# Scores ahead of the values product in each attention step of the first layer

## Chip, cores and metric

The kernel runs on one core of one Trainium2 chip. The metric is the device time of one execution in microseconds (us), lower is better. TensorE does the matrix products, ScalarE (ACT), VectorE (DVE) and GpSimd (POOL) the elementwise work, and each engine works through its own queue in program order, with semaphores between the queues.

## The reference, cut to what matters

Two layers run one after the other on x of shape (8, 32, 32, 512) in float32. The change touches only the first, a group norm, an attention with 8 heads of 64 channels over the 1024 positions of each of the 8 images, and an output projection with a residual:

```
qkv = group_norm(x) @ w_qkv + b_qkv            # (8, 1024, 1536)
weight = softmax(einsum('bhld,bhsd->bhls', q * scale, k * scale))
out = einsum('bhls,bhsd->bhld', weight, v)
x = x + out @ w_out + b_out
```

## The kernel before

`layer0` prepares weights and then runs the same block, `image`, for each of the 8 images. All products are made of pairs of a high and a low part of the float32 operands. TensorE first does the projections, then the attention, then the output projection of the image.

The attention of an image is a loop over steps `i_`. A **unit** u is 128 query rows of one head: 8 heads of 8 units, U = 64 units. Four functions issue TensorE's work:

- `scores(i_)` (L428, L429; called S here): 4 products of 512 columns into PSUM banks 2*(i_%2) and the next one. It waits for the exponentials of unit i_-2, which free these banks. At the first unit of a head it also waits for `staged`: POOL must have made the high and low parts of this head's keys and queries.
- `transposes(u)` with u = i_-2 (L443; T): 8 transposes of 128 columns, in two groups of four, into banks 4 and 5. Each group waits for `pl_ok`, which is DVE's subtraction of the group before it in the same bank.
- `output(b, part)` (L464; O): half of the values product of a pair b of units, 8 products of 256 columns. Part 0 runs in odd steps and begins with two more transposes, of the reciprocals of the row sums (L459; R). Part 1 runs in even steps and ends the pair's product (`av_ps`).

The other engines, in the order of their queues within step i_:

- ACT: in even steps two copies of the finished product of pair b = (i_-6)/2, `fold_t` (L544) and `fold_r` (L548), which wait for `av_ps`; then the high parts of the transposed probabilities of unit i_-2, `ph` (L558, two groups); then the exponentials of unit i_, `prob` (L565). In some steps a copy `ah` (L573).
- DVE: the row maximum of unit i_ (L599), which waits for its scores; in even steps the sum `fold_s` (L607), which waits for `fold_r`; the low parts `pl` of unit i_-2 (L616, two groups, each behind its `ph`); in odd steps the reciprocals (L620); in steps 23, 25, 39, 41, 55, 57 and four behind the last scores (`SPLIT_AT`) the low part `al` (L624), behind `ah`.
- POOL: for each pair the product `a_qk` (L696), behind `fold_s`. Behind this product of pairs 4k-2, 4k-1 and 4k, for k = 1 to 6, one of three parts of `stage(k + 1, ...)`. The last part, the low half of the keys `kl` (L687), follows pair 4k, so it lies in step 8k+6, and `scores(8k+8)`, the first of head k+1, waits for it:

```
for b in range(U // 2):
    pool.wait_ge(fold_add, b + 1)
    pool.tensor_tensor(qk[...], fold_s[...], fold_r[...], ALU.mult).then_inc(att_ok, 1)
    k, part = (b + 2) // NB, (b + 2) % NB
    if 1 <= k <= NH - 2 and part < 3:
        stage(k + 1, (part,))
```

(shortened; NB is 4.) SP's queue loads keys and queries of head h once the scores of head h-2 are done.

Of the kernel before, what the change touches and what calls it, by code (L numbers as in the profile page):

```python
# [80 lines left out]
def layer0(nc, x, gn_scale, gn_bias, w_qkv, b_qkv, w_out, b_out, x2, n_images=B):  # L81
    NB = TOK // 256
    U = NH * TT
    QSCALE = 1.0 / HD

    with ExitStack() as ctx:
# [275 lines left out]
        def image(i, after=None):  # L362

            with nc.Block() as block:
# [29 lines left out]
                def _(pe):  # L394

                    def projections(numbers):

                        for g in numbers:
                            if g >= 8:
                                pe.wait_ge(qk_sb, qk_upto[g - 7])  # L400
                                if v_upto[g - 7]:
                                    pe.wait_ge(vl_ok, v_upto[g - 7])
                            project(pe, g).then_inc(pr_ps, 1)

                    def turn(tiles):

                        if after is not None:
                            for t in tiles:
                                pe.wait_ge(x_ld[t], 16)
                                if t >= 4:  # L410
                                    pe.wait_ge(xt_sb, t - 3)
                                turn_tile(pe, t).then_inc(xt_ps, 1)

                    def scores(i_):

                        h, t = i_ // TT, i_ % TT
                        j = h % 2
                        if t == 0:
                            pe.wait_ge(staged, STAGE * (h + 1))
                        if i_ < 2:  # L420
                            pe.wait_ge(qk_sb, qk_upto[len(groups) - 8 + 2 * i_ + 2])
                        else:
                            pe.wait_ge(exp_ok, i_ - 1)
                        for kb in range(2):
                            bank = ps[:, 2 * (i_ % 2) + kb, :]
                            q_ = qs[:, j, t * P:(t + 1) * P]
                            n = slice(kb * 512, (kb + 1) * 512)
                            pe.matmul(bank, q_, kh[:, j, n], start=True, stop=False)  # L428
                            mm = pe.matmul(bank, q_, kl[:, j, n], start=False, stop=True)  # L429
                        mm.then_inc(score, 1)  # L430

                    def transposes(u):

                        pe.wait_ge(exp_ok, u + 1)
                        if u == 0:
                            pe.wait_ge(qk_sb, n_qk)
                        for g in range(2):
                            n = 2 * u + g
                            if n >= 2:
                                pe.wait_ge(pl_ok, n - 1)  # L440
                            for kk in range(4):
                                kt = 4 * g + kk
                                mm = pe.transpose(ps[:, 4 + n % 2, kk * P:(kk + 1) * P],  # L443
                                                  prob[:, u % 2, kt * P:(kt + 1) * P], ident[:])
                            mm.then_inc(tr_ps, 1)

                    def output(b, part):

                        h = b // NB
                        if part == 0:  # L450
                            pe.wait_ge(inv_ok, b + 1)
                            if b == 0:
                                pe.wait_ge(vl_ok, n_v)
                            if b >= 2:
                                pe.wait_ge(fold_add, b - 1)
                                pe.wait_ge(fold_cp, 2 * b - 2)
                            for n in range(2):
                                u = 2 * b + n
                                pe.transpose(ps[:, 6 + b % 2, 256 + n * P:256 + (n + 1) * P],  # L459
                                             row_inv[:, u:u + 1].to_broadcast([P, P]), ident[:])  # L460
                        pe.wait_ge(pl_ok, 4 * b + 3 + part)
                        for kt in range(4 * part, 4 * part + 4):
                            for e, q_ in enumerate((ph, pl)):
                                mm = pe.matmul(ps[:, 6 + b % 2, 0:256], v[:, h, kt, :], q_[:, b % 2, kt, :],  # L464
                                               start=kt == 0 and e == 0, stop=kt == TT - 1 and e == 1)
                        if part == 1:
                            mm.then_inc(av_ps, 1)

                    def out_tile(t):

                        if t == 0:
                            pe.wait_ge(pl_ok, 2 * U - 1)
                        elif t == 1:
                            pe.wait_ge(pl_ok, 2 * U)
                        elif t in (2, 3):
                            pe.wait_ge(fold_add, U // 2 + t - 3)
                            pe.wait_ge(fold_cp, U + 2 * (t - 3))
                        else:
                            pe.wait_ge(out_ok, t - 3)
                        n = slice(t * P, (t + 1) * P)  # L480
                        for k in range(CT):
                            if k == 0 and t == 0:
                                pe.wait_ge(ah_ok, SPLITS)
                                pe.wait_ge(al_ok, SPLITS)
                            if k == CT - 1 and t % 2 == 0:
                                pe.wait_ge(ah_ok, SPLITS + t // 2 + 1)
                                pe.wait_ge(al_ok, SPLITS + t // 2 + 1)
                            for e, (a, b) in enumerate(((ah[k][:, n], woh[:, k, :]), (ah[k][:, n], wol[:, k, :]),
                                                        (al[k][:, n], woh[:, k, :]))):
                                mm = pe.matmul(ps[:, 4 + t % 4, :], a, b, start=k == 0 and e == 0,  # L490
                                               stop=k == CT - 1 and e == 2)
                        mm.then_inc(out_ps, 1)
# [3 lines left out]
                    scores(1)  # L496
                    projections(range(len(groups) - LATE, len(groups)))
                    for i_ in range(2, U + 5):
                        if i_ >= 5:
                            output((i_ - 5) // 2, (i_ - 5) % 2)  # L500
                        if i_ < U:
                            scores(i_)
                        if i_ < U + 2:
                            transposes(i_ - 2)
                        if i_ in (U + 1, U + 2):
                            turn(range(2 * (i_ - U - 1), 2 * (i_ - U)))
                        if i_ == U + 3:
                            out_tile(0)
# [1179 lines left out]
```

## Time and profile before

| | |
|---|---|
| median of 3 runs | 4336.4 us (4334.82 to 4336.52) |
| the profiled execution, its own time | 4336.12 us |
| its span, first to last instruction | 4334.4 us |
| TensorE matmul busy | 4090.4 us, 94% |
| VectorE busy | 3034.6 us, 70% |
| ScalarE busy | 2526.4 us, 58% |
| GpSimd busy | 1299.5 us, 30% |
| mean granted TensorE clock | 0.983 of full speed |

The first layer takes a little over half of the span; the same pattern comes back for each image, about 293.6 us apart, from the first scores at 94.07 us (the last image begins its scores at 2145.07 us). Busy shares are means over stages with different limits. In a timeline, the start of one TensorE product to the start of the next is the time that it costs; the printed duration also holds the way through the array, so neighbouring products overlap, and an idle time in brackets is shorter than the time lost between starts.

### The profile page before, as it was taken

To read this page: it belongs to the slowest core of one execution; us is meant where nothing else is said; L and a number is where in the kernel's file an instruction comes from. 1 tells how busy PE (TensorE), PEld (TensorE's weight loads), DVE (VectorE), ACT (ScalarE), POOL (GpSimd) and SP (SyncE) were. 2 spreads that over 40 slices of the span, in tenths; PEclk is the share of its full clock that TensorE was granted. 3 is DMA by queue.
4 is the path that set the end of the run, shared out by engine and by line. 5 is a ranking of instruction groups with operands and counts; after the bars stand their busy time and mean duration, and the time that the engine had idled before them with its cause. 6 is when DMAs were issued, how large, how long until landed. Compare 5 with 4: busy or idle time off the path is not lost. (4 is left out here: it accounts for less than half of the span.)

```text
span 4334.4 us, 65337 instructions
## 1 busy us (share of the span) xinstructions
PE 4090.4 (94%) x22762; PEld 3392.0 (78%) x22762; DVE 3034.6 (70%) x5141; ACT 2526.4 (58%) x5502; POOL 1299.5 (30%) x1423
## 2 busy tenths in 40 slices
PE   8999999999999999999998998999999998989999
PEld 6888878878878788788787577777777777767777
DVE  3983966938839759478496567686776868676867
ACT  3864846838738558378385254454646463635545
POOL 1432432423324234223243014040413132231404
PEclk9999999999999999999999899999999999999999
DMA  2221221221211212212122121121303031212112
GB/s 81 50 64 35 60 68 30 50 59 40 66 42 40 73 36 59 60 30 64 44 50 90 60 58 60 35 77 25 86 13 98 21 73 45 59 59 54 64 36 63
DMA packets 113178, 236.10 MB, mean 54 GB/s; under 512 B 17260, under 2 KB 33704, under 8 KB 112808
## 3 DMA queue, kind: packets, MB, share of 16 engines
q1 hardware_dynamic: 112808, 231.41, 20.0%
q8 instruction: 203, 3.33, 0.3%
q14 instruction: 167, 1.37, 0.1%
HBM read 80.35 MB, written 33.55 MB: 26 GB/s over the span
## 5 line engine op out<-in xcount | busy, mean ns | idle before, releaser
L599 DVE TENSOR_REDUCE a_neg_max<-a_ps 128x1 f32<-128x1024 f32 x512 | 624.8, 1222 | 336.8 <-PE a_ps L429 336.8
L616 DVE TENSOR_TENSOR a_pl<-a_ps,a_ph 128x512 fp32r<-128x512 f32 x1024 | 654.5, 679 | 8.9 <-ACT a_ph L558 5.7
L558 ACT ACTIVATE a_ph<-a_ps 128x512 fp32r<-128x512 f32 x1024 | 556.7, 593 | 172.8 <-PE a_ps L443 169.9
L565 ACT ACTIVATE a_prob<-a_ps,a_neg_max 128x1024 f32<-128x1024 f32 x512 | 572.1, 1117 | 17.6 <-DVE a_neg_max L599 11.8
L696 POOL TENSOR_TENSOR a_qk<-a_fold_s,a_fold_r 64x256 f32<-64x256 f32 x256 | 191.1, 747 | 1235.9 <-DVE a_fold_s L607 1235.9
L1618 POOL TENSOR_SCALAR b_prob<-b_prob,b_row_inv 128x256 f32<-128x256 f32 x512 | 245.6, 480 | 1051.3 <-DVE b_row_inv L1536 1015.4
L443 PEld LDWEIGHTS a_ps<-a_ident,a_prob 128*128 128x128 f32 x4096 | 469.8, 140 | 112.6 <-issue 46.8
L443 PE MATMUL a_ps<-a_ident,a_prob 128*128 128x128 f32 x4096 | 540.8, 274 | 17.1 <-DVE a_pl L616 16.0
L464 PE MATMUL a_ps<-a_ph,a_v 128*128 128x256 f32 x2048 | 550.8, 302 | 0.0
L464 PE MATMUL a_ps<-a_pl,a_v 128*128 128x256 f32 x2048 | 509.2, 282 | 0.0
L428 PE MATMUL a_ps<-a_kh,a_qs 128*128 128x512 f32 x1024 | 408.4, 399 | 12.0 <-POOL a_kl L687 12.0
L429 PE MATMUL a_ps<-a_kl,a_qs 128*128 128x512 f32 x1024 | 404.7, 395 | 0.0
L464 PEld LDWEIGHTS a_ps<-a_pl,a_v 128*128 128x128 f32 x2048 | 389.4, 190 | 0.3
L464 PEld LDWEIGHTS a_ps<-a_ph,a_v 128*128 128x128 f32 x2048 | 386.7, 189 | 0.3
L1464 DVE SCALAR_TENSOR_TENSOR b_acc<-b_qpad,b_dww,b_acc 128x256 f32<-128x256 f32 x880 | 363.9, 481 | 4.9
L1313 ACT ACTIVATE b_diag<-b_ident,b_dww 128x128 f32<-128x128 f32 x656 | 250.7, 399 | 146.7 <-PE b_ps L1155 93.7
L1155 PE MATMUL b_ps<-b_qpad,b_diag 128*128 128x256 f32 x1312 | 324.1, 408 | 0.0
L1155 PEld LDWEIGHTS b_ps<-b_qpad,b_diag 128*128 128x128 f32 x1312 | 249.4, 190 | 72.9
L1390 ACT ACTIVATE b_prob<-b_ps,b_neg_max 128x256 f32<-128x256 f32 x512 | 235.8, 478 | 18.2 <-DVE b_neg_max L1541 18.2
L428 PEld LDWEIGHTS a_ps<-a_kh,a_qs 128*128 128x128 f32 x1024 | 193.6, 189 | 43.8 <-POOL a_kl L687 21.7
L594 DVE TENSOR_TENSOR a_v<-a_ps,a_v 128x512 fp32r<-128x512 f32 x64 | 44.3, 692 | 245.2 <-ACT a_v L527 245.2
L429 PEld LDWEIGHTS a_ps<-a_kl,a_qs 128*128 128x128 f32 x1024 | 194.2, 190 | 24.9
(249 smaller groups left out, 9232.8 us busy)
## 6 DMA issues: line engine op xcount, KB each, us to landing
a_qs<-a_qk SPq DMA_DIRECT2D x128, 256.0 KB, 3.7
a_kl<-a_qk SPq DMA_DIRECT2D x128, 256.0 KB, 4.3
a_xtok<-in_x SPq DMA_DIRECT2D x64, 256.0 KB, 4.0
b_xs<-x SPq DMA_DIRECT2D x64, 256.0 KB, 5.1
b_qs<-b_qh SPq DMA_DIRECT2D x64, 256.0 KB, 3.0
b_qs<-b_ql SPq DMA_DIRECT2D x64, 256.0 KB, 3.8
b_z<-x SPq DMA_DIRECT2D x64, 256.0 KB, 3.1
out<-b_ot SPq DMA_DIRECT2D x64, 256.0 KB, 2.0
```

Of the source, the lines that this page charges most:

```text
L428: pe.matmul(bank, q_, kh[:, j, n], start=True, stop=False)
L429: mm = pe.matmul(bank, q_, kl[:, j, n], start=False, stop=True)
L443: mm = pe.transpose(ps[:, 4 + n % 2, kk * P:(kk + 1) * P], prob[:, u % 2, kt * P:(kt + 1) * P], ident[:])
L464: mm = pe.matmul(ps[:, 6 + b % 2, 0:256], v[:, h, kt, :], q_[:, b % 2, kt, :], start=kt == 0 and e == 0, stop=kt == TT - 1 and e == 1)
L558: act.activation(ph[:, b % 2, 4 * g:4 * g + 4, (u % 2) * P:(u % 2 + 1) * P], ps[:, 4 + n % 2, :].rearrange("p (k q) -> p k q", k=4), ACT.C ...
L565: act.activation(prob[:, i_ % 2, :], ps[:, 2 * (i_ % 2):2 * (i_ % 2) + 2, :] .rearrange("p a b -> p (a b)"), ACT.Exp, bias=neg_max[:, i_:i ...
L599: dve.tensor_reduce(neg_max[:, i_:i_ + 1], ps[:, 2 * (i_ % 2):2 * (i_ % 2) + 2, :] .rearrange("p a b -> p (a b)"), AX, ALU.max, negate=Tru ...
L616: dve.tensor_tensor(pl[here], ps[:, 4 + n % 2, :].rearrange("p (k q) -> p k q", k=4), raw(ph[here]), ALU.subtract).then_inc(pl_ok, 1)
L1155: mm = pe.matmul(ps[:, c, 0:NS], diag[:, e % DIAGS, :], src, start=first, stop=last)
L1313: act.activation(diag[:, e % DIAGS, :], ident[:], ACT.Copy, scale=dww[:, c, n:n + 1])\
L1464: dve.scalar_tensor_tensor(dst, src, dww[:, c, n:n + 1], dst, ALU.mult, ALU.add)\
L1618: pool.tensor_scalar(prob[:, u % 2, t, :], prob[:, u % 2, t, :], row_inv[:, c:c + 1], 0.0, ALU.mult, ALU.add).then_inc(sc_ok, 1)
```

## The change

In each step of the loop `scores(i_)` is issued first, then the half of the values product, then the transposes. No instruction is added or removed, and the queues of the other engines keep their order.

```diff
                     for i_ in range(2, U + 5):
+                        if i_ < U:
+                            scores(i_)
                         if i_ >= 5:
                             output((i_ - 5) // 2, (i_ - 5) % 2)
-                        if i_ < U:
-                            scores(i_)
                         if i_ < U + 2:
                             transposes(i_ - 2)
```

## Rows read from the trace of the kernel before

**Rows 1.** Windows: length, PE, PEld, DVE, ACT, POOL busy us, clock, DMA share, GB/s

```profile
107.95:282.33 174.38, 171.92 (x1242) 155.50 (x1240) 159.33 (x242) 152.34 (x301) 68.86 (x59) 1.00 0.21 49
333.00:340.00 7.00, 2.39 (x7) 1.75 (x6) 0.00 (x0) 2.30 (x4) 0.00 (x0) 0.70 0.04 9
```

**Rows 2.** TensorE's waits over the whole span: total us, times, longest

```profile
PE a_ps L443 <- DVE a_pl L616: 16.0, 48, 0.6
...
PE a_ps L428 <- POOL a_kl L687: 12.0, 48, 0.3
```

**Rows 3.** Timeline of TensorE, steps 14 to 16: start us, us, work, [idle <-releaser]

```profile
134.65 0.40 PE L428 MATMUL a_ps<-a_kh,a_qs 128*128 128x512 f32 x1
...
135.58 1.03 PE L443 MATMUL a_ps<-a_ident,a_prob 128*128 128x128 f32 x8
136.45 0.38 PE L459 MATMUL a_ps<-a_ident,a_row_inv 128*128 128x128 f32 x2
...
137.62 0.40 PE L428 MATMUL a_ps<-a_kh,a_qs 128*128 128x512 f32 x1
...
140.86 0.50 PE L428 MATMUL a_ps<-a_kh,a_qs 128*128 128x512 f32 x1 [0.32 <-POOL a_kl L687]
```

**Rows 4.** Timeline of TensorE: transposes ahead of scores in step 3; 512-column products around a values product

```profile
102.36 1.06 PE L443 MATMUL a_ps<-a_ident,a_prob 128*128 128x128 f32 x8
...
103.49 0.39 PE L429 MATMUL a_ps<-a_kl,a_qs 128*128 128x512 f32 x1
...
294.04 0.39 PE L490 MATMUL a_ps<-wout_hi,a_al_last 128*128 128x512 f32 x1
...
295.22 0.40 PE L490 MATMUL a_ps<-wout_hi,a_a 128*128 128x512 f32 x1
```

**Rows 5.** Timeline of ACT, steps 13 and 14, and behind the last values product

```profile
133.46 1.08 ACT L558 ACTIVATE a_ph<-a_ps 128x512 fp32r<-128x512 f32 x2 [0.69 <-PE a_ps L443]
134.43 1.13 ACT L565 ACTIVATE a_prob<-a_ps,a_neg_max 128x1024 f32<-128x1024 f32 x1
...
135.66 0.38 ACT L544 ACTIVATE a_fold_t<-a_ps 64x256 f32<-64x256 f32 x1
...
295.42 0.38 ACT L544 ACTIVATE a_fold_t<-a_ps 64x256 f32<-64x256 f32 x1 [4.53 <-PE a_ps L464]
```

**Rows 6.** Timeline of DVE, steps 13 and 14

```profile
134.16 1.28 DVE L616 TENSOR_TENSOR a_pl<-a_ps,a_ph 128x512 fp32r<-128x512 f32 x2
135.36 0.15 DVE L620 RECIPROCAL a_row_inv<-a_row_sum 128x2 f32<-128x2 f32 x1
135.78 1.23 DVE L599 TENSOR_REDUCE a_neg_max<-a_ps 128x1 f32<-128x1024 f32 x1 [0.27 <-PE a_ps L429]
137.03 0.43 DVE L607 TENSOR_TENSOR a_fold_s<-a_ps,a_fold_t 64x256 f32<-64x256 f32 x1
```

**Rows 7.** Timeline of POOL, step 14

```profile
137.60 0.74 POOL L696 TENSOR_TENSOR a_qk<-a_fold_s,a_fold_r 64x256 f32<-64x256 f32 x1 [2.88 <-DVE a_fold_s L607]
138.42 2.38 POOL L687 TENSOR_TENSOR a_kl<-a_kl,a_kh 128x1024 fp32r<-128x1024 f32 x1
```

**Rows 8.** Timeline of TensorE: first scores of head 3 (step 24), transposes of steps 25 and 27

```profile
164.21 0.50 PE L428 MATMUL a_ps<-a_kh,a_qs 128*128 128x512 f32 x1 [0.18 <-POOL a_kl L687]
...
168.30 1.16 PE L443 MATMUL a_ps<-a_ident,a_prob 128*128 128x128 f32 x8
...
174.64 1.16 PE L443 MATMUL a_ps<-a_ident,a_prob 128*128 128x128 f32 x8 [0.33 <-DVE a_pl L616]
```

**Rows 9.** Timeline of DVE, from the end of step 25 into step 26

```profile
171.75 0.69 DVE L624 TENSOR_TENSOR a_a<-a_qk,a_a 128x512 fp32r<-128x512 f32 x1 [0.59 <-ACT a_a L573]
172.36 1.22 DVE L599 TENSOR_REDUCE a_neg_max<-a_ps 128x1 f32<-128x1024 f32 x1
173.49 0.41 DVE L607 TENSOR_TENSOR a_fold_s<-a_ps,a_fold_t 64x256 f32<-64x256 f32 x1
173.82 0.67 DVE L616 TENSOR_TENSOR a_pl<-a_ps,a_ph 128x512 fp32r<-128x512 f32 x1
```

## The prediction

> **What bounds the kernel now.** I read the windows first, then TensorE's waits, then the timelines step by step. From step 5 of an image to its last scores, 174.38 us, TensorE is busy for 171.92 us, while DVE with 159.33 and ACT with 152.34 follow closely [rows 1]. So TensorE sets the pace of the attention, and a new order of the same instructions can only change its idle time. That idle time has two sources: the transposes wait 48 times for `pl` and the scores 48 times for POOL's `kl`, six of each per image [rows 2]. The scores' waits are at the first unit of heads 2 to 7.
>
> TensorE's own costs, start to start: S is 0.93 (134.65 to 135.58), T 0.87 (135.58 to 136.45), and R with O 1.17 (136.45 to 137.62) [rows 3]. A 512-column product (0.23) and an O behind it take 1.18 [rows 4], so O is 0.95 and R 0.22. An even step costs 0.93 + 0.95 + 0.87 = 2.75, an odd one 2.97, a pair 5.72. Without a wait the scores of step 16 would have begun at 137.62 + 2.75 = 140.37; they began at 140.86 [rows 3]. This 0.49 is lost for good, since everything else keeps up. For heads 3, 5 and 7 the printed idle time is 0.14 smaller [rows 3, 8], so they lose 0.35.
>
> **Part one: the same work in a new order, 0.** The order S, T, O becomes S, O, T. The new neighbours are S to O, O to T and T to S. The 1.18 from which I took O already holds two such switches, 512 columns into O and O into 512 columns [rows 4]. T straight into S takes 1.13 up to S's second product, against 0.87 + 0.23 = 1.10, with a short wait within T [rows 3, 4]. O into T has the last switch of the 1.18 as its nearest case. I take 0 and, for the range, 0.01 us either way in each of some 500 steps, 5 us.
>
> **Part two: does TensorE begin to wait in ordinary steps? No.** I lay out a pair of steps in the new order, with 0 at the start of an even step's S. TensorE: S at 0, O 0.93 to 1.88, T 1.88; then S 2.75, R 3.68, O 3.90, T 4.85; and at 5.72 the next pair.
>
> ACT first. `ph` begins 0.63 behind T's start: 133.46 against 134.65 - 0.95 - 0.87 = 132.83. The exponentials follow 0.97 later and hold ACT for 1.23, from 134.43 to 135.66 [rows 3, 5]. `fold_t` can begin 0.20 behind the end of O: 295.42 against 295.22 [rows 4, 5]. In the even step it does so at 2.08; `fold_r`, also 0.38 long, ends at about 2.86; `ph` begins at 2.8, the exponentials at 3.77, and ACT is free at 5.0. In the odd step: `ph` at 5.48, exponentials 6.45, free at 7.68, just before the next `fold_t` at 7.80.
>
> DVE next. Its maximum can begin 1.13 behind S (135.78 against 134.65), and the next operation comes 1.13 later (172.36 to 173.49); `pl` needs 0.70 behind its `ph` (134.16 against 133.46), and its two groups hold DVE for 1.20 [rows 3, 5, 6, 9]. Even step: `pl` from 3.50 to 4.70. The odd maximum begins at 4.70, where 3.88 would be possible; `pl` at 6.18, reciprocals at 7.38, which hold DVE 0.15 less the 0.08 by which its operations overlap (171.75 + 0.69 against 172.36) [rows 9]. The next maximum is at 7.45, 1.73 in the even step, instead of 1.13.
>
> What TensorE needs: scores at 5.72 want the exponentials of 5.0, spare 0.7. Transposes at 4.85 want the first `pl`, ended at 4.17; their second group, half a T later at 5.29, wants 4.78, spare 0.5. Between the end of `pl` and a released T lie 0.15 (173.82 + 0.67 against 174.64) [rows 8, 9], so 0.35 remains as the least. Ordinary steps stay at 5.72 a pair. At the start of the loop there is no O until step 5, and T of step 63 stands at the same place in TensorE's queue in both orders, as does all behind it. Both ends cost 0.
>
> **Part three: the staging for the next head comes late, +30 us.** This is the price of the change. In step 8k+6 a chain runs from the end of O over `fold_t`, `fold_r`, `fold_s`, `a_qk` and `kl` to the scores of step 8k+8. Before, O stood ahead of S, its result waited for ACT, and `fold_t` began 135.66 - 134.65 = 1.01 behind S [rows 3, 5]. Now O ends later than that, and `fold_t` begins at 2.08.
>
> Heads 2, 4, 6: `fold_s` began 1.25 behind the maximum [rows 6], now 1.73 + 1.25 = 2.98, and ends at 3.41; `a_qk` 0.14 later at 3.55; `kl` 0.82 later at 4.37, ending after 2.38 at 6.75; the scores 0.06 later (140.80 to 140.86) at 6.81 [rows 3, 6, 7]. Against 5.72 they lose 1.09, before 0.49: growth 0.60. Heads 3, 5, 7: the sum starts right behind `fold_r` at 2.90 and takes 0.41 [rows 9]; by the same distances `kl` ends at 6.65 and the scores begin at 6.71. They lose 0.99, before 0.35: growth 0.64.
>
> Per image 3 x 0.60 + 3 x 0.64 = 3.72, in 8 images 29.8 us. If the handoffs of ACT and DVE in this chain are off by 0.15, which is the one that I could read (`pl` to T), it is 48 x 0.15 = 7 us either way. O, now queued behind the waiting scores, and T behind it are only shifted with them.
>
> **Part four: steps behind a split, -5 us.** S of step 24 starts at 164.21, its first product 0.10 longer than usual; with 0.93 + 0.10 + 0.87 + 1.17 + 0.93 T of step 25 was due at 168.21 and began at 168.30, and itself took 1.16 instead of 1.03: 0.22 lost. From there T of step 27 was due at 168.30 + 0.13 + 0.87 + 0.95 + 3.90 = 174.15 and began at 174.64: with another 0.13, 0.62 lost [rows 3, 8]. In the new order the longer stall of step 24, 0.64 more, lets DVE finish the split of step 23, and the 0.22 goes. Behind the split of step 25 the chain is longer: the exponentials of an odd step move from 134.43 - 134.65 = -0.22 [rows 3, 5] to 6.45 - 5.72 = 0.73 of the next even step, and `al` hangs on them. It was at 171.75, or 1.50 of step 26 (170.25), and moves to 2.45; the maximum to 3.06, `pl` to 4.52, its end to 5.19 [rows 9]. T, due at 4.85, begins at 5.34 and loses 0.49 + 0.13, as before. Net 0.22, three times per image: 0.22 x 3 x 8 = 5.3 us. Bounds: 0 and twice this.
>
> **Sum.** 29.8 - 5.3 = +24.5 us. From the profiled 4336.12 that is 4360.6, and the median of the runs is 0.3 above that execution: **4361 us**, +0.6%. A difference under 0.2%, 8.7 us, can hardly be told from none.
>
> **Rivals.** *Faster (0.05).* T comes 0.95 later behind its step's scores. If DVE has `pl` done by then even behind a split, and `kl` is no later than now, T's waits behind splits vanish: 3 x (0.22 + 0.62) x 8 = 20 us, 4316 us. For it: 48 such waits exist [rows 2]. Against: `ph`, and so `pl`, hang on the same later T. It decides if the scores of step 16 still lose no more than 0.49.
>
> *No change (0.09).* The chain to `kl` keeps its place behind S, because ACT and not O sets `fold_t`; then only the 0.22 terms move, and it is 4331 to 4337 us. For it: before, ACT set it. Against: ACT is free at 7.68 - 5.72 = 1.96, and O's result comes at 2.08.
>
> *Transposes wait in each pair (0.09).* The least spare is 0.35. If handoffs take 0.45 more than I place them, 0.1 is lost in each of some 29 pairs of 8 images: +23 us, 4384 us. For it: DVE has little idle time left, 174.38 - 159.33 = 15 us over 29 pairs [rows 1].
>
> *The clock falls (0.03).* In a stretch with TensorE busy for 2.39 of 7.00 us its granted clock was 0.70 on average, between its levels of 1.2 and 2.4 GHz, so 4.2 us of it at the lower one; in the attention it stayed at 1.00 in spite of the waits of 0.32 us [rows 1, 3]. If each of the 48 stalls, now about 1 us, brought such 4.2 us, half of them would be lost: 48 x 2.1 = 101 us, 4462 us. The Trainium skill, "TensorE: Matmul & The Clock Gate", section "A second HAM failure mode: psum-queue depth-cycling", says that short idle times between groups of products, if frequent, can make the clock swing between its levels; by that rule this rival would come true. The trace before has such idle times and no swing.
>
> **How the numbers follow.** The forecast has 0.74. Its own range is 24.5 with 5 for part one, 7 for part three and 5 for part four, some 12 together: 4349 to 4373. I widen it to 4345 to 4380, towards no change and towards waiting transposes, so that about 2 in 10 stay outside. Slower by over 0.2%: 0.74 + 0.09 + 0.03, less 0.01 for a forecast that comes out very small, 0.85; within 0.2% 0.10; faster 0.05.
>
> **What would show it.** The wait of the scores for `kl` should print near 0.9 and 0.8 instead of 0.32 and 0.18, 48 times, some 42 us in all instead of 12. `fold_t` should begin 2.1 behind S and be released by O. Ordinary pairs stay at 5.72. T of step 25 waits no more, T of step 27 about as long. I am wrong if T waits in ordinary pairs, or if `kl` comes no later behind its S.

## The result and the profile after

The changed kernel takes 4361.64 us, the median of 4 runs (4360.12 to 4363.06); the kernel before takes 4336.46 us beside it. The ratio is 1.0059, with a 95% interval of 1.0041 to 1.0076. A second measurement of the same kernel gave 4361.76 against 4336.05 us, 1.0058 (1.0044 to 1.0072). So the change costs 25 us, 0.6%, by the medians; between the two profiled executions, 4363.06 and 4336.12 us, it is 27 us. The forecast was 4361 us.

TensorE's waits over the whole span of the changed kernel, total us, times and longest, answer to [rows 2]:

```profile
PE a_ps L428 <- POOL a_kl L687: 39.1, 48, 0.9
...
PE a_ps L443 <- DVE a_pl L616: 16.8, 40, 0.7
```

The 48 first scores of a head now wait 39.1 us for POOL's `kl`, where they waited 12.0. The transposes wait 40 times instead of 48, for about the same total. Of the five waits of an image that are left, three are those of T in steps 27, 43 and 59, behind a split, and two lie at the loop's ends; before, it was the same three and three at the ends. The timeline of TensorE of the changed kernel, from the scores of step 14 to those of step 17, answers to [rows 3]:

```profile
134.38 0.47 PE L428 MATMUL a_ps<-a_kh,a_qs 128*128 128x512 f32 x1
...
136.33 1.04 PE L443 MATMUL a_ps<-a_ident,a_prob 128*128 128x128 f32 x8
137.12 0.47 PE L428 MATMUL a_ps<-a_kh,a_qs 128*128 128x512 f32 x1
137.44 0.39 PE L429 MATMUL a_ps<-a_kl,a_qs 128*128 128x512 f32 x1
...
138.12 0.38 PE L459 MATMUL a_ps<-a_ident,a_row_inv 128*128 128x128 f32 x2
...
139.29 1.03 PE L443 MATMUL a_ps<-a_ident,a_prob 128*128 128x128 f32 x8
141.17 0.50 PE L428 MATMUL a_ps<-a_kh,a_qs 128*128 128x512 f32 x1 [0.84 <-POOL a_kl L687]
...
143.94 0.48 PE L428 MATMUL a_ps<-a_kh,a_qs 128*128 128x512 f32 x1
```

The order within a step is S (137.12), R and O (138.12), T (139.29). The scores of step 16 should have begun 2.97 behind those of step 15, at 140.09, and began at 141.17: 1.08 lost. Then 0.02 more, since step 16 took 2.77 (141.17 to 143.94) for 2.75.

ACT, DVE and POOL in the same steps, answering to [rows 5 to 7]:

```profile
136.53 0.38 ACT L544 ACTIVATE a_fold_t<-a_ps 64x256 f32<-64x256 f32 x1
136.93 0.38 ACT L548 ACTIVATE a_fold_r<-a_ps 64x256 f32<-64x256 f32 x1
```

```profile
136.13 1.20 DVE L599 TENSOR_REDUCE a_neg_max<-a_ps 128x1 f32<-128x1024 f32 x1
137.37 0.43 DVE L607 TENSOR_TENSOR a_fold_s<-a_ps,a_fold_t 64x256 f32<-64x256 f32 x1
```

```profile
137.93 0.74 POOL L696 TENSOR_TENSOR a_qk<-a_fold_s,a_fold_r 64x256 f32<-64x256 f32 x1 [2.76 <-DVE a_fold_s L607]
138.75 2.37 POOL L687 TENSOR_TENSOR a_kl<-a_kl,a_kh 128x1024 fp32r<-128x1024 f32 x1
```

The scores of step 14 began at 134.38, an even step of 2.75 (here 2.74) ahead of 137.12. Counted from them, `fold_t` begins at 2.15 (before 1.01, forecast 2.08), the maximum 1.75 (forecast 1.73), `fold_s` 2.99 (2.98), `a_qk` 3.55 (3.55), `kl` 4.37 (4.37), ending at 6.74 (6.75). The timetable of the prediction is there to 0.1 us.

A clean measure of the attention alone is the **stretch** of an image: from its first scores (step 0) to its last transposes (step 63), two products that stand at the same places of TensorE's queue in every kernel here. Both ends for the first image, in the kernel before and in the changed one:

```profile
94.07 0.39 PE L428 MATMUL a_ps<-a_kh,a_qs 128*128 128x512 f32 x1
...
286.65 0.30 PE L443 MATMUL a_ps<-a_ident,a_prob 128*128 128x128 f32 x1 [0.61 <-DVE a_pl L616]
```

```profile
94.86 0.39 PE L428 MATMUL a_ps<-a_kh,a_qs 128*128 128x512 f32 x1
...
290.16 0.30 PE L443 MATMUL a_ps<-a_ident,a_prob 128*128 128x128 f32 x1 [0.68 <-DVE a_pl L616]
```

192.58 us became 195.30 us, and the other seven images repeat this within 0.06 us. Eight times 2.72 is 21.8 us of the 25 to 27.

### The profile page after: what moved, and what is told of

The parts are those of the page before. It is cut to its first block and busy times, and to the rows that moved or that the text cites. A ratio compares the mean times of both kernels' runs of the same rounds, so it can differ in the third digit from the quotient of the medians.

```text
span 4361.3 us, 65337 instructions
## 1 busy us (share of the span) xinstructions
PE 4086.8 (94%) x22762; PEld 3405.8 (78%) x22762; DVE 3035.8 (70%) x5141; ACT 2524.5 (58%) x5502; POOL 1300.0 (30%) x1423
## 5 line engine op out<-in xcount | busy, mean ns | idle before, releaser
L464 PE MATMUL a_ps<-a_ph,a_v 128*128 128x256 f32 x2048 | 529.5, 292 | 0.0
L443 PEld LDWEIGHTS a_ps<-a_ident,a_prob 128*128 128x128 f32 x4096 | 456.8, 140 | 41.8 <-issue 35.2
L428 PE MATMUL a_ps<-a_kh,a_qs 128*128 128x512 f32 x1024 | 444.7, 434 | 39.1 <-POOL a_kl L687 39.1
```

Of the source, the lines that this page charges most:

```text
L443: mm = pe.transpose(ps[:, 4 + n % 2, kk * P:(kk + 1) * P], prob[:, u % 2, kt * P:(kt + 1) * P], ident[:])
```

## Experiments

Six of the eight kernels of the first two rounds pair the two orders, so that each edit is seen under both.

**e1 and e2: `kl` one pair earlier.** Its stage part moves from pair 4k to pair 4k-1, in the new order (e1) and in the old one (e2):

```diff
-                        if 1 <= k <= NH - 2 and part < 3:
-                            stage(k + 1, (part,))
+                        if 1 <= k <= NH - 2 and part < 2:
+                            stage(k + 1, (0,) if part == 0 else (1, 2))
```

> The new order, with POOL's last staging part (kl) made one pair earlier, in step 8k+4. Late-staging theory: the 48 first scores of a head no longer wait, which gives back 3 x (1.10 + 1.06) x 8 = 52 us; the transposes of step 25 and its like wait again for 0.22, 5 us. About 4315 us. Rival, that the new order itself costs TensorE time (switches between kinds of products, or transposes waiting in many steps): the waits for kl go here too, but e1 stays some 25 us above e2.

> The old order with the same earlier kl. Late-staging theory: 3 x (0.60 + 0.45) x 8 = 25 us less than before, about 4311 us, and so within some 5 us of e1: without the wait for kl the order makes no difference. Rival, that the order itself costs time: e1 minus e2 is the 25 us of the change.

Measured: e1 4327.9 us, ratio 0.9980 (0.9971 to 0.9989); e2 4332.4 us, ratio 0.9989 (0.9980 to 0.9998). The waits for `kl` are gone in both and the change's 25 us with them; the new order is, if anything, ahead. That is for late staging and against a price of the order itself. Both gained less than expected, which was 4315 and 4311 us: they missed by 13 and 21 us. One reason shows in TensorE's waits for `pl`, of e1, now 64 instead of 40:

```profile
PE a_ps L443 <- DVE a_pl L616: 24.8, 64, 0.7
```

and in e2's timeline at steps 25 and 26:

```profile
165.94 0.40 PE L428 MATMUL a_ps<-a_kh,a_qs 128*128 128x512 f32 x1
...
167.41 1.16 PE L443 MATMUL a_ps<-a_ident,a_prob 128*128 128x128 f32 x8 [0.37 <-DVE a_pl L616]
...
169.35 0.40 PE L428 MATMUL a_ps<-a_kh,a_qs 128*128 128x512 f32 x1
```

Step 25 in the old order should take 2.75 and takes 3.41: 0.66 lost behind the split of step 23, not the 0.22 seen before [rows 8]. The wait for `kl` in step 24 had hidden the rest. e1 loses as much there: 0.67 in step 25 and 0.62 in step 27.

**e3 and e4: only the first step of each head.** e3 is the new order with the old one in steps 8, 16, ... 56; e4 is the opposite. Both are shown as an edit of the changed kernel.

```diff
+                        late = i_ % TT == 0        # e4: i_ % TT != 0
-                        if i_ < U:
+                        if i_ < U and not late:
                             scores(i_)
                         if i_ >= 5:
                             output((i_ - 5) // 2, (i_ - 5) % 2)
+                        if i_ < U and late:
+                            scores(i_)
```

> The new order, but in the first step of each head (steps 8, 16, ... 56) the values product still goes ahead of the scores. Theory that the scores of a head's first unit are wanted 0.95 us too early: kl, done 6.75 behind the scores of step 14, meets scores due at 5.72 + 0.95 = 6.67, so 0.14 and 0.04 are lost instead of 1.10 and 1.06; 47 us less, 5 us back for the transposes of step 25: about 4320 us. Rival, that the loss is made in steps 8k+6 by the later fold, or spread over all steps: only a small part comes back, 4350 us or more.

> The old order, but in the first step of each head the scores go first. Same theory: kl is done 6.15 (6.01) behind the scores of step 8k+6, and the scores that want it are due at 5.72 - 0.95 = 4.77, so 1.44 (1.30) is lost instead of 0.60 (0.45): 3 x 1.69 x 8 = +41 us, less 5 us for the transposes of step 25, about 4372 us, slower than the full change though only 6 of 61 steps per image are changed. Rival, loss spread over all steps or made by the later fold of step 8k+6: a tenth of the change, about 4339 us.

Measured: e3 4332.3 us, ratio 0.9989 (0.9980 to 0.9998); e4 4386.9 us, ratio 1.0118 (1.0103 to 1.0134). Expected were 4320 and 4372 us, so e3 is 12 and e4 15 us above its number; the rivals' 4350 us or more and 4339 us are further off. In e3 the whole loss is gone although 52 of the 59 steps in which the order can matter keep the new one; a part of the gain that was expected is missing because the split of step 23 costs 0.54 in step 25 and not 0.22. In e4 seven steps per image cost nearly twice what the whole change costs. In e4's timeline the scores of step 16 follow straight behind T of step 15 and wait longest:

```profile
136.37 0.40 PE L428 MATMUL a_ps<-a_kh,a_qs 128*128 128x512 f32 x1
...
139.57 0.50 PE L428 MATMUL a_ps<-a_kh,a_qs 128*128 128x512 f32 x1 [1.24 <-POOL a_kl L690]
```

3.20 where 0.93 + 0.87 = 1.80 is due: 1.40 lost, 1.44 expected. So what costs is that a head's first scores are asked for 0.95 us of TensorE's work sooner. The later fold of step 8k+6, seen from the scores, is the same fact from the other side. From the start of T in step 14, `kl` even ends sooner in the new order, after 4.79 us (136.33 to 141.12) instead of 5.22 (135.58 to 140.80 [rows 3, 7]). That is 0.43 sooner, where the scores want it 0.95 sooner; the 0.52 between the two is the growth of the loss.

**e5 to e8: the splits in quarters.** To take the waits behind the splits away under both orders, each half of 512 columns became two quarters in odd steps, with DVE's part one step later; e5 and e6 have the early `kl` of e1 and e2 as well, e7 and e8 have not.

```diff
-        SPLIT_AT = {16 * c + 23 + 2 * s: (c, slice(s * HALF, (s + 1) * HALF)) ... for s in range(2)}
+        SPLIT_AT = {16 * c + 23 + 2 * s: (c, slice(256 * s, 256 * s + 256)) ... for s in range(4)}
-        SPLITS = 2 * (CT - 1)
+        SPLITS = 4 * (CT - 1)
-                        if i_ in SPLIT_AT:                     # VectorE
-                            c, n = SPLIT_AT[i_]
+                        at = i_ if i_ >= U else i_ - 1
+                        if at in SPLIT_AT:
+                            c, n = SPLIT_AT[at]
```

> New order, kl one pair early, and the splits in quarters of 256 columns in four odd steps, VectorE's half of each one step later, behind its pl. Theory: what e1 still loses per image is 1.29 us behind each of three pairs of splits; with these gone the stretch from an image's first scores to its last transposes falls from 190.62 to about 186.75 us, which is 31 us over 8 images: about 4297 us, if the stretches between images stay. Rival, that the transposes wait for another reason (pl late in general in the new order): the stretch stays near 190.

> Old order with the same two edits. Theory: the stretch falls from 190.83 to about 186.96 us, about 4301 us, and equals that of e5 within 0.3 us, because nothing is left for the order to change. Rival, that the new order has a cost or gain of its own: the two stretches differ by more.

> New order, the splits in quarters as in e5, kl at its old place. Theory: the stretch goes from 195.28 to 193.24 us (three waits of 0.68 go), perhaps 0.2 more per head start where ScalarE's quarter copy of step 29 now lies ahead of the fold copies of step 30. About 4346 us.

> Old order, the splits in quarters, kl at its old place. Theory: the stretch goes from 192.58 to about 190.0 us (three times 0.23 and 0.62 go). e7 minus e8 is then the price of the late staging alone, about 3.2 us per image; that full change shows 2.70 because its longer waits for kl hide the 0.22 waits behind the splits. Rival, that the 0.22 and 0.62 do not come from the splits: e7 minus e8 stays at 2.70.

Measured: e5 4307.5 us, ratio 0.9933 (0.9919 to 0.9946); e6 4307.2 us, 0.9932 (0.9918 to 0.9945); e7 4364.4 us, 1.0065 (1.0051 to 1.0078); e8 4361.0 us, 1.0053 (1.0039 to 1.0066). All four missed. e5 and e6 are 10 and 6 us short of their numbers. Their medians are equal, but their stretches, 188.40 and 188.93 us, are 0.53 apart where 0.3 was allowed, so by the stretch the new order is 4 us ahead; 0.24 of the 0.53 arises in steps 28 and 44, which lose 0.18 in e5 and 0.30 in e6. e7's stretch was to fall to 193.2 and rose to 196.2, e8's was to fall to 190.0 and rose to 194.4 us. With that, e7 minus e8 says nothing on the price of the late staging. DVE in its steps 24 and 30 of e8, and POOL in step 30, tell why:

```profile
168.82 0.41 DVE L625 TENSOR_TENSOR a_a<-a_qk,a_a 128x256 fp32r<-128x256 f32 x1
...
187.24 2.27 DVE L625 TENSOR_TENSOR a_a<-a_qk,a_a 128x256 fp32r<-128x256 f32 x1
189.43 1.21 DVE L599 TENSOR_REDUCE a_neg_max<-a_ps 128x1 f32<-128x1024 f32 x1
```

```profile
186.84 2.38 POOL L688 TENSOR_TENSOR a_kl<-a_kl,a_kh 128x1024 fp32r<-128x1024 f32 x1
```

The subtraction took 0.41 us in step 24, with POOL idle. In step 30 it took 2.27: `kl` ended at 189.22 and the subtraction 0.29 behind it, as if it had stood still until POOL's operation was over. In e7 the same one took 2.23 to 2.25. In e5 and e6 the subtraction met POOL's `TENSOR_SCALAR` in the staging, in two of the four steps of the first two groups, and took 0.99 to 1.13. DVE and POOL of e6:

```profile
172.19 1.13 DVE L625 TENSOR_TENSOR a_a<-a_qk,a_a 128x256 fp32r<-128x256 f32 x1
```

```profile
171.99 1.05 POOL L676 TENSOR_SCALAR a_kh<-a_qs 128x1024 fp32r<-128x1024 f32 x1
```

**e9 and e10: the quarters apart from POOL.** As e5 and e6, with the quarters of the first two groups at steps 16c + 23, 29, 31 and 37:

```diff
-        SPLIT_AT = {16 * c + 23 + 2 * s: ...
+        SPLIT_AT = {16 * c + 23 + ((0, 6, 8, 14) if c < 2 else (0, 2, 4, 6))[s]: ...
```

> As e5, but the quarters of the first two groups lie at steps 16c+23, 29, 31 and 37, so that VectorE's quarter never runs beside a TENSOR_SCALAR of POOL's staging (in e5 and e6 its 0.42 us became 1.0 to 1.13 us there). Theory, that these two engines block each other: every wait behind a split goes and the stretch of an image falls from 188.40 to about 186.7 us, 14 us in all, about 4294 us. Rival, that quarters are simply too many operations for VectorE: the waits stay, whichever steps the quarters are in, and it is near 4307 us.

> The same in the old order. Theory: the stretch falls from 188.91 to about 186.9 us, about 4292 us, equal to e9 within what can be measured: with the staging early and the splits apart the order of scores and values product does not matter. Rival: a difference of 10 us or more between the orders.

Measured: e9 4293.4 us, ratio 0.9904 (0.9889 to 0.9919); e10 4299.7 us, 0.9914 (0.9901 to 0.9928). e9 was expected at 4294 and e10 at 4292 us, so e9 met its number and e10 is 8 us above. Each quarter now takes 0.41 to 0.42 in the steps before the last scores. TensorE's waits of e9 have no line for `kl`, and of the transposes' waits three per image are left, at the loop's ends:

```profile
PE a_ps L444 <- DVE a_pl L617: 8.7, 24, 0.5
```

These two beat both kernels of the study by about 1%. The medians of e9 and e10 are 6 us apart, and their intervals overlap; by the stretches, 186.79 and 187.11, it is 2.6 us over the eight images.

**e11 and e12: the two kernels of the study again.**

> The changed kernel once more, for a second profile and a firmer ratio. If the 5 us that it lost outside the attention's stretch belong to the change, the stretches between images are longer again in this profile; if they come from where the low-clock pieces fall, they differ from the first profile. The stretch of an image stays at 195.3 us and the time near 4361 us.

> The kernel before once more, profile only: its stretch of 192.58 us per image repeats, and the stretches between images show how much they vary without any change (100.9 to 102.5 us in the first profile).

Measured: e11 4361.8 us; e12, a single run, 4336.6 us. Their stretches repeat, 195.33 and 192.61, and so do the lengths between the images, told below: 705.0 and 702.7 us in sum.

**All kernels by the stretch of the first image**, taken from TensorE's timelines, against 8 times the difference to 192.58 and against the difference of the medians (before beside each: 4336.5, 4337.0 for e1 to e4, 4336.0 for e5 to e11):

| kernel | stretch, us | 8 x difference | medians | left over |
|---|---|---|---|---|
| after | 195.30 | +21.8 | +25.2 | +3 |
| e11, after again | 195.33 | +22.0 | +25.7 | +4 |
| e1 new, kl early | 190.63 | -15.6 | -9.1 | +7 |
| e2 old, kl early | 190.83 | -14.0 | -4.5 | +9 |
| e3 new, head start old | 191.16 | -11.4 | -4.7 | +7 |
| e4 old, head start new | 197.59 | +40.1 | +49.9 | +10 |
| e5 new, early, quarters | 188.40 | -33.4 | -28.5 | +5 |
| e6 old, early, quarters | 188.93 | -29.2 | -28.8 | 0 |
| e7 new, quarters | 196.16 | +28.6 | +28.4 | 0 |
| e8 old, quarters | 194.37 | +14.3 | +25.0 | +11 |
| e9 new, quarters apart | 186.79 | -46.3 | -42.7 | +4 |
| e10 old, quarters apart | 187.11 | -43.8 | -36.3 | +7 |

What is left over lies outside the stretches. The windows between the last transposes of an image and the first scores of the next hold the same work in all kernels (length, TensorE, weight loads, DVE, ACT, POOL busy, granted clock, DMA share and GB/s). Image 2 to 3 of the kernel before, image 4 to 5 of the changed one, and image 3 to 4 of e4:

```profile
581.76:682.66 100.90, 93.07 (x428) 76.53 (x429) 33.62 (x56) 25.58 (x42) 29.41 (x21) 0.97 0.21 58
```

```profile
1181.42:1283.26 101.84, 93.98 (x428) 77.13 (x429) 33.61 (x56) 25.59 (x42) 29.44 (x21) 0.97 0.20 58
```

```profile
889.05:991.84 102.79, 94.55 (x428) 77.62 (x429) 33.62 (x56) 25.58 (x42) 29.45 (x21) 0.95 0.20 57
```

They differ by 0.9 and 1.9 us, and in e4 the granted clock was 0.95 instead of 0.97. The 0.9 of the changed kernel came at the same 0.97, and no run here explains it. Summed over the seven, they are 702.9 us before, 706.3 after and 711.3 in e4.

One pattern is in the timelines. From the first scores of an image to those of the next it takes 293.5 to 293.8 us in the kernel before (images 2 to 6), and 293.3 to 293.7 in e2, whose stretch is 1.75 us shorter: between the images e2 then takes 102.5 to 102.8 us at a granted clock of 0.95, where the kernel before takes 100.9 to 101.2 at 0.97. These periods are 296.9 to 297.2 us in e8 and mostly 297.1 to 297.2 in the changed kernel, with stretches of 194.4 and 195.3. So a gain in the attention can be given back between the images; of the 9 us left over in e2 and the 11 in e8, 8 lie there. Why is not shown.

## Why the prediction was right

**The bound.** TensorE sets the pace, and only its idle time moved: its busy time is 4086.8 us against 4090.4 before. e9 and e10 confirm it from below, since with the waits gone both orders run at TensorE's sum: each step from 6 on is 2.75 or 2.97 us.

**Part one, 0 for the new order.** Right. S to O to T to S costs 2.75 and 2.97 as before. The 0.08 by which S's first product starts early behind T (137.12 to 137.44 is 0.32 instead of 0.23) is made up by an early start.

**Part two, no waits in ordinary steps.** Right: from step 5 to step 15 not one wait of the transposes is left between starts, and `fold_t`, released by the end of O, and DVE's maximum lie within 0.1 us of the timetable. The rival of waiting transposes falls.

**Part three, +30 us.** The mechanism is the one that was named, and e1, e3 and e4 show it by three different edits. The size was 11% too large. The new loss of 1.10 (1.09 forecast) is right, but the old one was read as 0.49, and it is 0.60: in the kernel before, the scores of step 17 follow those of step 16 at 143.94,

```profile
143.94 0.40 PE L428 MATMUL a_ps<-a_kh,a_qs 128*128 128x512 f32 x1
```

3.08 instead of 2.97, since the first product behind a wait runs 0.10 longer. I counted this tenth in part four and forgot it in part three. For heads 3, 5 and 7 the new loss is also 0.05 more than the forecast 0.99 (their wait prints 0.80), so their growth was near 0.6, as forecast. The sum is 3 x (0.50 + 0.61) x 8 = 27 us for 30.

**Part four, -5 us.** Nearly right, 4 us for 5. T of step 25 no longer waits, T of step 27 still does:

```profile
172.80 1.04 PE L443 MATMUL a_ps<-a_ident,a_prob 128*128 128x128 f32 x8
...
176.31 1.16 PE L443 MATMUL a_ps<-a_ident,a_prob 128*128 128x128 f32 x8 [0.39 <-DVE a_pl L616]
```

The first gives 0.22 back, as forecast. The second loses 0.68 in step 27, where the forecast kept 0.62 as before, so the part is 3 x 0.16 x 8 = 4 us. 27 - 4 = 23 us stands against 22 in the stretches; the last 1 us is gained by ordinary steps, some of which take 2.74 for 2.75. But the 0.22 was not the whole price of a split, as I had read it. e1 and e2 show 0.66 where no wait for `kl` goes ahead, so the wait in step 24 had paid two thirds of it before the change. Waits in one queue hide each other, and a sum of waits taken away one by one promises too much: I expected 25 us of e2 on this ground, and its stretch gave 14.

**What part of the 25 us was not forecast.** The forecast of 24.5 was met by 22 in the attention and some 3 between the images. That second part was not in the prediction, and made it look better than it was: that the total fits to 1 us is luck. Between the first seven images the same work takes 100.3 to 102.9 us over the kernels here, and where it takes longest the granted clock over it is 0.95 and not 0.97 or 0.98. The second profiles have 705.0 us there in the changed kernel instead of 706.3, and 702.7 in the kernel before instead of 702.9, so it comes with the change in every pairing, with 2 to 4 us. Whether the stretch's length sets them in a way that could be foretold was not tested.

**The rivals.** No gain appeared from T's later place, since `pl` follows T. The 48 waits that the prediction held for this rival were in fact half at the loop's ends: only 24 of them, the T of steps 27, 43 and 59 in each image, lay behind splits. The chain did not keep its place behind S. As for the clock, over steps 4 to 63 of the first image, with six stalls of 1.1 us in them, the changed kernel has

```profile
105.00:286.00 181.00, 174.54 (x1262) 159.63 (x1262) 163.66 (x248) 155.81 (x307) 68.72 (x59) 1.00 0.21 49
```

a granted clock of 1.00, so these stalls do not bring it down.

## What to carry to other kernels

Where one engine is full, a new order of its queue is worth only what it does to the few places that wait for another engine: lay one period out as a timetable, and ask at which point of the queue each result is wanted, not only when it is made. Before adding up waits as a gain, ask which of them lie in the shadow of another, by an experiment that takes the first one away. When two orders lie within 0.2% of each other once the waits are gone, as e9 and e10 do, the lever was elsewhere: moving one POOL operation and placing the pieces of one VectorE operation gave 36 to 43 us in either order.

## What the runs showed of the hardware

- VectorE and GpSimd shut each other out. A VectorE subtraction with both inputs in SBUF, 0.41 us alone, took 0.99 to 1.13 us when it began within a GpSimd `TENSOR_SCALAR` and 2.27 us within a `TENSOR_TENSOR` of 2.38 us; it ended 0.27 to 0.29 us behind the GpSimd operation each time. The other way round it holds as well: the GpSimd product `a_qk` that begins 0.1 us into such a subtraction behind the last scores of an image (291.05 and 290.94 in the kernel before) took 0.92 us instead of 0.74. The larger `pl` subtractions with one input in PSUM kept their 0.68 us beside the same GpSimd work. The Trainium skill, "GPSIMD Engine Reference", section "1. Specifications", has the rule that VectorE operations with two SBUF inputs contend with GpSimd for the SBUF interface; the runs agree, and show that the cost is the whole rest of the GpSimd operation and not a slower rate. What an operation costs VectorE thus depends on the step that it is put in, more than on its size.
- The same work between two of the first seven images took 100.3 to 102.9 us, with a granted clock of 0.98 to 0.95 over it; between the last two it took 95.3 to 97.0 us, at 1.00 or 0.98. Edits far away, in the attention, moved what lies outside the stretches by 0 to 11 us, 8.4 of e4's 10 in these windows, so a change of a few us in a kernel of this kind has to be read from its own stretch of the trace.
